# Attention with relative positions in a four-block network on one core: stage 1 double-buffered, parts stored once, batches side by side in the position tables

## What is computed

```python
x = x + L0_attn(_layernorm(x))      # B 8, S 512, H 256, 16 heads of d 16
def L0_attn(hidden_states, ..., rel_embeddings, Wq, bq, Wk, bk, Wv, bv, Wo, bo, ...):
    q = split_heads(hidden_states @ Wq + bq); k, v likewise
    scores = einsum('bhqd,bhkd->bhqk', q, k) / scale
    pos_k = (rel_embeddings @ Wk + bk)                      # 128 buckets, per head
    c2p_att = einsum('bhqd,hpd->bhqp', q, pos_k)            # gathered at c2p_pos(q - k)
    p2c_att = einsum('bhkd,hpd->bhkp', k, pos_k)            # gathered at p2c_pos, transposed
    scores = scores + (c2p + p2c) / scale
    ctx = softmax(scores) @ v
```

## Time and profile before

| | us |
|---|---|
| runs, median of 3 | 2948.34 (2947.35 to 2954.58) |
| the profiled execution's own time | 2920.05 |
| its span | 2918.4 |
| PE busy | 1966.0 |
| DVE busy | 1921.8 |
| ACT busy | 1234.3 |
| POOL busy | 939.9 |
| DMA moved | 492.63 MB, 169 GB/s over the span |

### The profile page before, as it was taken

The page is one execution under the profiler, slowest core; times in us unless marked ns, Lnnn a source line. Parts: engine busy times, 40 slices in busy tenths (PEclk is TensorE's granted clock), DMA queues, the critical chain, the costliest instruction groups (busy, mean ns, idle before and its releaser), DMA issues. The chain is left out here.

```text
span 2918.4 us, 47884 instructions
## 1 busy us (share of the span) xinstructions
PE 1966.0 (67%) x13524; PEld 1442.7 (49%) x13525; DVE 1921.8 (66%) x4329; ACT 1234.3 (42%) x2141; POOL 939.9 (32%) x1177
## 2 busy tenths in 40 slices
PE   4452677777777777777763888867613515999963
PEld 2231466555565655566552656644312502888631
DVE  5652688777787878788874666618774775444454
ACT  2332666666666666666640232224300115333200
POOL 3222222222222222222222221114774001555576
PEclk8776799999999999899986999988756555999986
DMA  4666988888888989889964121000000141444644
GB/s 136 210 204 179 292 274 284 269 275 276 265 287 273 288 271 291 267 273 289 294 184 110 43 58 29 0 20 0 0 0 2 59 165 40 154 155 151 126 131 124
DMA packets 208344, 492.63 MB, mean 169 GB/s; under 512 B 39169, under 2 KB 104353, under 8 KB 208129
## 3 DMA queue, kind: packets, MB, share of 16 engines
q1 hardware_dynamic: 179392, 420.25, 45.5%
q0 software_dynamic: 24576, 57.11, 7.9%
q10 hardware_dynamic: 4160, 12.58, 1.1%
HBM read 248.45 MB, written 241.30 MB: 168 GB/s over the span
## 5 line engine op out<-in xcount | busy, mean ns | idle before, releaser
L816 DVE CUSTOM_DVE_ANT_0 probs<-bank,c2p 128x512 f32<-128x512 f32 x512 | 551.5, 1077 | 231.8 <-PE bank L711 154.5
L789 ACT COPY a_stage<-bank 128x320 f32<-128x320 f32 (+1 forms) x512 | 364.5, 712 | 275.2 <-PE bank L679 269.2
L773 ACT ACTIVATE probs<-probs,neg_max 128x512 f32<-128x512 f32 x512 | 363.6, 710 | 22.5 <-DVE neg_max L816 22.0
L692 PE MATMUL bank<-tab,k 96*128 96x320 bf16 (+1 forms) x512 | 160.8, 314 | 286.1 <-DVE b_stage L767 227.8
L825 DVE COPY probsT<-bank 128x512 f32<-128x512 f32 x512 | 351.6, 687 | 2.5 <-PE bank L721 2.5
L721 PE MATMUL bank<-ident,probs 128*128 128x128 f32 x2048 | 326.5, 284 | 4.1 <-ACT probs L773 3.9
L721 PEld LDWEIGHTS bank<-ident,probs 128*128 128x128 f32 x2048 | 261.4, 148 | 18.4 <-issue 6.2
L711 PE MATMUL bank<-ident,p2c 128*128 128x128 f32 x1280 | 263.9, 307 | 0.0
L2017 POOL DMA_INDIRECT p_x_tile<-y_d,p_token x160 | 152.5, 953 | 328.2 <-POOLq L1708 208.2
L655 POOL COPY end_c2p<-a_stage 128x4 f32<-128x4 f32 (+1 forms) x128 | 24.1, 188 | 721.3 <-ACT a_stage L789 571.6
L767 ACT COPY b_stage<-bank 128x288 f32<-128x288 f32 (+1 forms) x256 | 186.3, 728 | 151.9 <-PE bank L692 150.9
(11 more groups left out here) (252 smaller groups left out, 3931.3 us busy)
## 6 DMA issues: line engine op xcount, KB each, us to landing
p2c_d<-b_stage SPq DMA_DIRECT2D x64, 640.0 KB, 3.6
c2p_d<-a_stage SPq DMA_DIRECT2D x64, 640.0 KB, 3.4
p2c_d<-b_stage SPq DMA_DIRECT2D x64, 576.0 KB, 7.8
c2p_d<-a_stage SPq DMA_DIRECT2D x64, 576.0 KB, 5.8
p2c<-p2c_d SPq DMA_DIRECT2D x256, 144.0 KB
c2p<-c2p_d SPq DMA_DIRECT2D x256, 144.0 KB, 5.9
o_sorted_d<-p_o_pair SPq DMA_DIRECT2D x80, 256.0 KB, 2.3
q_stack_d<-p_parts SPq DMA_DIRECT2D x96, 128.0 KB
```

What stands on the lines that cost most here:

```text
L692: pe.matmul(bank[B_BANK][:, x0:x1], k6[:, g, j * S + t * P:j * S + (t + 1) * P], tab6[:, w // 8, 1, x0:x1], start=True, stop=True).then_in ...
L773: act.activation(probs[:, w % 2, j, :], probs[:, w % 2, j, :], ACT.Exp, bias=neg_max[:, w % 2, j:j + 1], scale=-1.0).then_inc(exp_done, 1)
L789: act.copy(a_stage[:, wa % 2, x0:x1, j], bank[A_BANK][:, x0:x1]).then_inc(a_copied, 1)
L816: dve.tensor_tensor_reduce(probs[:, w % 2, j, :], bank[S_BANKS[(HB * w + j) % 3]][:], c2p[:, w % 2, :, j], -SCALE, LOWEST, ALU.add, ALU.mi ...
```

## The change

Stage 1 is written out for the eight batches with two sets of nT, full and parts and four of x. q and k are stored once, as three parts per chunk in one DMA ([H * D, 3, B * S] in HBM), all by SP. The third product goes. In its place the far bias is computed for all heads at once by a product of k with a matrix of the table's end columns, masked by head (`w_far`, FAR_BANK), split into three parts, two batches together, and stored (`far_stack_d`). In stage 2 these six numbers per key are six more rows of k6 (96 to 102); q6 has ones or zeros there, which POOL writes once at the start (`picks`), since a query tile in the first half of a batch has its far keys on one side and one in the second half on the other. The six slots are now put together at load time: `load_quarter` issues three DMAs of 16 rows per unit, and one of the six far rows in one unit of four. The first group is loaded by SP, the second by ACT.

In a_stage, b_stage, c2p, p2c and the HBM tables the four batches lie side by side ([HB, TABLE] in place of [TABLE, HB]). Tables are always 320 columns wide (before, 288 for the first and last tile of a batch).

```diff
-        q_stack_d = dram("q_stack_d", [H, STACK, D, B * S], BF16)
-        qf_stack_d = dram("qf_stack_d", [H, STACK, D, B * S], BF16)
-        k_stack_d = dram("k_stack_d", [H, STACK, D, B * S], BF16)
+        q_stack_d = dram("q_stack_d", [H * D, 3, B * S], BF16)
+        k_stack_d = dram("k_stack_d", [H * D, 3, B * S], BF16)
+        far_stack_d = dram("far_stack_d", [H, FAR, B * S], BF16)
         c2p_stack_d = dram("c2p_stack_d", [H, STACK, D, TABLE], BF16)
         p2c_stack_d = dram("p2c_stack_d", [H, STACK, D, TABLE], BF16)
-        c2p_d = dram("c2p_d", [4, P, TABLE, B // 2], F32)
-        p2c_d = dram("p2c_d", [4, P, TABLE, B // 2], F32)
+        c2p_d = dram("c2p_d", [4, P, B // 2, TABLE], F32)
...
-            x_in = sb(st, "p1_x", [P, 2, TPB, C])
+            x_in = sb(st, "p1_x", [P, 4, TPB, C])
             normed = sb(st, "p1_normed", [P, 2, TPB, C])
-            nT = sb(st, "p1_nT", [P, CC, S])
+            nT = sb(st, "p1_nT", [P, 2, CC, S])
...
-            full = sb(st, "p1_full", [P, CH, S])
-            rest = sb(st, "p1_rest", [P, CH, S])
-            parts = sb(st, "p1_parts", [P, CH, 3, S], BF16)
+            full = sb(st, "p1_full", [P, 2, CHUNKS, S])
+            rest = sb(st, "p1_rest", [P, CHUNKS, S])
+            parts = sb(st, "p1_parts", [P, 2, CHUNKS, 3, S], BF16)
+            far_rest = sb(st, "p1_far_rest", [4 * H, S])
+            far_parts = sb(st, "p1_far_parts", [4 * H, 3, S], BF16)
...
-            def store_stack(eng, stack_d, part_sb, m, cols, done, order):
-
-                heads = H // CC
-                for slot, part in enumerate(order):
-                    eng.dma_start(stack_d[m * heads:(m + 1) * heads, slot, :, cols], part_sb[:, part, :]
-                                  ).then_inc(done, 16)
-            Q_ORDER, K_ORDER = (0, 1, 2, 0, 1, 0), (0, 0, 0, 1, 1, 2)
+            Y_BANKS, M_BANKS, V_BANK, FAR_BANK = (0, 1), (2, 3, 4, 5), 6, 7
+
...
+                        for m in range(CHUNKS):
+                            sp.wait_ge(parts_ready, CHUNKS * b + m + 1)
+                            sp.dma_start((q_stack_d, k_stack_d)[m // CC][m % CC * P:(m % CC + 1) * P, :, b * S:(b + 1) * S],
+                                         parts[:, u, m]).then_inc(parts_stored[u], 16)
+                        if u:
+                            sp.wait_ge(far_split, b // 2 + 1)
+                            for v in range(2):
+                                for side in range(2):
+                                    rows = (2 * v + side) * H
+                                    sp.dma_start(far_stack_d[:, 3 * side:3 * side + 3, (b - 1 + v) * S:(b + v) * S],
+                                                 far_parts[rows:rows + H]).then_inc(far_stored, 16)
                     for u in range(2):
...
-                            pe.wait_ge(v_ready, 2 * b + j + 1)
+                            wait_count(pe, v_ready, 2 * b + j)
                             for s in (2 * j, 2 * j + 1):
                                 for c in range(CC):
-                                    last = pe.matmul(bank[6 + j][:, (s % 2) * C:(s % 2 + 1) * C],
-                                                     nT[:, c, s * P:(s + 1) * P], wv[:, c, :],
+                                    last = pe.matmul(bank[V_BANK][:, (s % 2) * C:(s % 2 + 1) * C],
+                                                     nT[:, u, c, s * P:(s + 1) * P], wv[:, c, :],
                                                      start=c == 0, stop=c == CC - 1)
                             last.then_inc(v_projected, 1)
-                    each_batch(pe, body)
...
+                        pe.wait_ge(full_ready, CHUNKS * (b + 1))
+                        if b == 0:
+                            pe.wait_ge(w_far_ready, 1)
+                        if u == 0:
+                            wait_count(pe, far_left, b // 2)
+                        for c in range(CC):
+                            last = pe.matmul(bank[FAR_BANK][2 * H * u:2 * H * (u + 1), :], w_far[:, c, :],
+                                             full[:, u, CC + c, :], start=c == 0, stop=c == CC - 1)
+                        last.then_inc(far_made, 1)
 
...
+                    for b in range(B):
+                        split(b, 0)
+                        split(b, 1)
+                        if b + 2 < B:
+                            moments(b + 2)
+                        split(b, 2)
+                        split(b, 3)
+                        if b + 2 < B:
+                            normalize(b + 2)
                         for j in range(2):
...
-            q6 = sb(st, "q6", [STACK * D, 4, 2, HB * S], BF16)
-            k6 = sb(st, "k6", [STACK * D, 4, HB * S], BF16)
+            q6 = sb(st, "q6", [STACK * D + FAR, 4, HB * S], BF16)
+            k6 = sb(st, "k6", [STACK * D + FAR, 4, HB * S], BF16)
+            NEAR_K = slice(0, STACK * D)
...
-            a_stage = sb(st, "a_stage", [P, 2, TABLE, HB])
-            b_stage = sb(st, "b_stage", [P, 2, TABLE, HB])
-            c2p = sb(st, "c2p", [P, 2, S, HB])
+            a_stage = sb(st, "a_stage", [P, 2, HB, TABLE])
+            b_stage = sb(st, "b_stage", [P, 2, HB, TABLE])
+            c2p = sb(st, "c2p", [P, 2, HB, S])
...
-            p2c = sb(st, "p2c", [P, TPB, NEAR, HB])
+            p2c = sb(st, "p2c", [P, TPB, HB, NEAR])
...
+            def load_quarter(eng, r, h, half, slot):
+
+                tokens = slice(half * HB * S, (half + 1) * HB * S)
+                stack, stack_d, order = ((k6, k_stack_d, K_ORDER), (q6, q_stack_d, Q_ORDER))[r // 2]
+                for row in range(r % 2 * STACK // 2, (r % 2 + 1) * STACK // 2):
+                    eng.dma_start(stack[row * D:(row + 1) * D, slot], stack_d[ds(h * D, D), order[row], tokens]
+                                  ).then_inc(group_loaded[slot], 16)
+                if r == 1:
+                    eng.dma_start(k6[STACK * D:, slot], far_stack_d[ds(h, 1)].rearrange("h k n -> (h k) n")[:, tokens]
+                                  ).then_inc(group_loaded[slot], 16)
+            GROUP_LOADS = 16 * (2 * STACK + 1)
...
-                            skew = bass.AP(table_d.tensor, ((slot * P + ROWS * g) * TABLE + ROWS - 1 - ROWS * g + j0) * HB,
-                                           [[(TABLE - 1) * HB, ROWS], [1, (j1 - j0) * HB]])
-                            sp.dma_start(dest[g * ROWS:(g + 1) * ROWS, j0 + left:j1 + left, :].rearrange("p n b -> p (n b)"),
-                                         skew).then_inc(done, 16)
+                            skew = bass.AP(table_d.tensor, (slot * P + ROWS * g) * HB * TABLE + ROWS - 1 - ROWS * g + j0,
+                                           [[HB * TABLE - 1, ROWS], [TABLE, HB], [1, j1 - j0]])
+                            sp.dma_start(dest[g * ROWS:(g + 1) * ROWS, :, j0 + left:j1 + left], skew).then_inc(done, 16)
...
-                        if w % TPB == 0 and is_unit(i, w) and is_unit(*ahead(i, w, 2 * TPB)):
-                            load_group(2 * i + w // 8 + 1, (w // TPB) % 2, (w // TPB + 2) % 4)
+                        if is_unit(i, w) and is_unit(*ahead(i, w, 2 * TPB)):
+                            load_quarter(sp, w % TPB, 2 * i + w // 8 + 1, (w // TPB) % 2, (w // TPB + 2) % 4)
...
-                            sp.dma_start(c2p_d[wa % 4, :, x0:x1, :].rearrange("p n b -> p (n b)"),
-                                         a_stage[:, wa % 2, x0:x1, :].rearrange("p n b -> p (n b)")).then_inc(a_written[wa % 2], 16)
+                            sp.dma_start(c2p_d[wa % 4], a_stage[:, wa % 2]).then_inc(a_written[wa % 2], 16)
...
-                            return pool.tensor_copy(dest[:, c0:c1, :], ends_of[:, side, :].unsqueeze(1).broadcast_to(
-                                [P, c1 - c0, HB]))
+                            return pool.tensor_copy(dest[:, :, c0:c1], ends_of[:, side, :].unsqueeze(2).broadcast_to(
+                                [P, HB, c1 - c0]))
...
+                    picks = q6[STACK * D:].rearrange("k g (b t n) -> k (g b) t n", b=HB, t=2)
+                    pool.wait_ge(ones_set, 1)
+                    pool.memset(q6[STACK * D:], 1.0).then_inc(far_set, 1)
+                    for half, base, sign in ((0, 3, -1), (1, -2, 1)):
+                        pool.wait_ge(far_set, half + 1)
+                        pool.affine_select(out=picks[:, :, half], in_=picks[:, :, half], compare_op=ALU.is_gt, fill=0.0,
+                                           base=base, pattern=[[0, 4 * HB], [0, S // 2]], channel_multiplier=sign
+                                           ).then_inc(far_set, 1)
+                    pool.wait_ge(far_set, 3)
...
-                        pe.matmul(sc[:, near], q6[:, g, 0, own], k6[:, g, j * S + lo * P:j * S + (hi + 1) * P],
+                        pe.matmul(sc[:, near], q6[NEAR_K, g, own], k6[NEAR_K, g, j * S + lo * P:j * S + (hi + 1) * P],
                                   start=True, stop=False, skip_group_check=True)
```

(10 more changed lines are left out.)

326 lines of the change are left out of this document (165 added, 161 removed).

## The result

The changed kernel takes 2835.07 us (median of 4 runs, 2822.17 to 2839.59); the kernel before, beside it, 2951.46 (2947.35 to 2955.20). The ratio is 0.9607, 95% interval 0.9575 to 0.9639: 116 us faster, where 194 were forecast. The time lies inside the forecast range, on the side of rival (a). The profiled execution took 2822.17 us.

A forecast was written before the change was run, and what follows sets the result against it. It took the sync queue's stores to pace stage 1, and DMA in load units alternating with a chain in the others to bound stage 2. -88 + 8 - 114 = -194 from 2920, plus 28, gave 2755 us; range 2670 to 2880.

The forecast's parts named there:

- rival (a): Stage 2 table reads: smaller pieces cost the DMA engines more, so stage 2 gains only 8 us; 2860 us, chance 0.12.
- Stage 1: Projections, splitting, storing: fewer stores and no third product leave the DVE-PE loop as pace; 182 us against 274, taken as -88.
- Filling: Start of stage 2: PE waits until POOL has written the six selection rows; +8 us, bounds 0 and +20.
- Addition and copies: Stage 2 engines: without the four-float stride, score additions take 700 ns for 1079, b copies 485 for 719, a copies near 450.
- Units of stage 2: Attention of layer 0, 128 units of four score tiles: 8.5 us each for 9.39, -114 us.
- three bounds, 7.0, 8.0 and 7.8: Stage 2, us per unit: engines (DVE with its wait for PE), the chain over two units, and DMA; together 8.2.
- plus 0.33: Stage 2, us per unit: the stall at the loop's end in every sixteenth unit, which stays.
- the DMA bound of 7.8: Stage 2: 2.58 MB per unit at 333 GB/s, spread evenly over the units, takes 7.8 us.
- the forecast's own bounds: Limits without rivals: stage 1 -115 to -48, unit 8.0 to 8.8 us, fill 0 to 20; 2695 to 2840 us.
- Rival (c): Stage 2 sync queue: reads may cost 1.09 us each to issue, 10.6 us per unit; 3023 us, chance 0.08.
- Rival (b): Stage 2: engines set the pace, DMA does not; unit 7.0 + 0.33 us, -264 for -114; 2605 us, chance 0.07.
- Rival (d): Stage 2: the addition stays at 1079 ns; moves the forecast under 30 us; chance 0.72 together with the forecast.

The follow-up runs named there:

- the interleaved kernel: The changed kernel with the table layout of before, the four batches of a column side by side again; 2848.08 us, ratio to before 0.9654.
- the short reloads: The changed kernel with reloads of q, k and far rows cut from 2048 tokens to 128 after the first loop body; ratio to before 0.9576.

## Why the prediction was right and wrong

**Stage 1: right.** Stage 2's first instruction starts at 187.2 us for 274.1: -87, forecast -88. That close a hit is in part luck: the sum on record ended at 182, which is -92, and -88 was taken without a reason. A batch takes about 20 us (first q activation 21.5, last 167.3, seven batches and a chunk), forecast 19.5, and the first split starts at 22.9, forecast 24. The loop is the one named: in 48 to 189 us DVE's v addition waits 24.5 us for PE, and PE and its weight loads 33 to 36 for that addition. The store took 543 ns for the 360 assumed, without effect at four per batch.

**Filling: right.** Memset and selects took 6.9 and 7.5 us for 7.6 and 7.6; PE starts 15.6 us after the stage's first instruction, forecast 16. From that first instruction to the first addition it is 38.4 us in all for 31.9: +6.5, forecast +8.

**Addition and copies: right.** 691 ns for 700, 481 for 485, 427 for 450.

**Units of stage 2: the failed term, -42 for -114.** The step was "three bounds, 7.0, 8.0 and 7.8, lie close; together ... 8.2", plus 0.33. Its direction held and its size did not, for two reasons. First, the sync queue was taken as open: the 3.25 issues more were put "where the queue otherwise waits for ACT". But that wait was 3.2 us of a unit of 9.39; 1.4 for the loads came out of it, and the unit was to be 0.9 shorter at the same time. Had I summed the queue as I summed the engines (9.39 - 3.2 + 1.4 = 7.6 with the old issue times), there would have been a fourth bound close to the others. It would still not have been the largest. It measured 9.06 - 0.5 = 8.5, since the issues themselves became slower: p2c reads at 498 ns in the median for 431, some groups of four at 3.73 us for 2.67. By the sums over 1000 us the queue issues some 2.1 us more per unit, of which 1.1 are the loads and 0.75 the same eight reads. Second, the DMA bound of 7.8 rested on the 333 GB/s of one load unit. Over 1000 us the interleaved kernel gives 281 GB/s at 0.91, 309 at full share, and the changed one 285 at 0.96, 297: 8.4 and 8.7 us for 2.58 MB. Rival (a) thus was real (0.3 us per unit) and was smaller than the misreading of the rate. Its sign, a share of 1.0 at less than 300 GB/s, nearly shows (0.96 at 285), and 2835 us is nearer to its 2860 than to the forecast; the short reloads, which take 6% of the bytes away for under 1% of the time, are what speaks against it as the cause.

Shown: adding time to the queue lengthens the unit nearly one for one (1.2 us gave 0.93, three issues 1.18), while fewer bytes move it by 0.1 or less, and the other layout, which trades DVE's time against the cost of the reads, by 0.2. Not shown: what the unit would be with the queue relieved, since each of the three kernels that relieved it made loads late, crowded them on few engines, or took the time from ACT. A relief that issues the last quarter earlier, or merged loads with 16 rows outermost, wasn't tried. So it stays open how much of 9.06 the queue holds alone, and whether the DMA engines at 0.96 would have stopped the unit at 8.7.

**The total.** A unit of 9.06 us lies outside the forecast's own bounds (8.0 to 8.8), and two thirds of the gain in stage 2 didn't come. The time still lies 5 us inside the bounds that the forecast gave itself (2840), because stage 1 and the filling used none of the room, 40 and 12 us, that was left for them. That is luck and not a merit of the bounds for stage 2.

Rival (c), the queue as the slower end, had the right resource at the wrong price: reads at 0.43 to 0.50 us, not 1.09. Rival (b) had units of 7.3 us and fell with 9.06. Rival (d) fell with the 691 ns. No kernel tried that does the whole computation beats the changed one.

## What to carry to other kernels

Sum the queue that issues DMAs like an engine: its issues by its rows, its waits as its only slack, and compare both with the unit you forecast, not with the one you have. Take a bandwidth for a sum from a long window, at its busy share, not from the best unit. Before you move or merge a load, write down when it must land and over how many DMA engines its outermost dimension spreads it.
